# A vision-transformer block: one projection for two groups of tokens, factor products by high and low parts, and a new order of the steps

## The chip, the cores and the metric

The kernel runs on one core of a Trainium2 chip. The metric is the device time of one execution in microseconds (us), lower is better. The engines are TensorE (PE, with its weight loads as PEld), VectorE (DVE), ScalarE (ACT), GpSimd (POOL) and SyncE (SP), which issues most DMAs. A measurement of this kernel can tell about 0.5% from no change.

## The reference

The block takes 32 images of 3x96x96. It cuts each into 36 patches of 768 numbers, projects them to 256 (with a class token: 37 tokens an image, 1184 in all), applies a factored attention, and then a mixture of 8 experts of which each token takes 2. Cut to what matters:

```python
h = concat([cls, patches @ W.T + b], 1) + pos_enc                  # 32 x 37 x 256
x = layernorm(h)
Q, K, Z = x @ Wq.T, x @ Wk.T, cumsum(x, 1) / counts
bil = (Q @ V_b) * cumsum(K @ W_b, 1) @ U_b.T
tri = (Q @ V_t) * (Z @ X_t) * cumsum(K @ W_t, 1) @ U_t.T
h = h + ((bil + alpha * tri) / counts + bias_b + alpha * bias_t) @ Wo.T
x = layernorm(h)
gates = softmax(x @ w_router + b_router)                           # top 2 of 8, 185 places an expert
out = gelu(buf @ w1 + b1) @ w2 + b2                                # for each expert
h = h + weighted sum of each token's two experts, weights divided by their sum
```

## The kernel before

**Groups.** The 1184 tokens lie in ten tiles of 128 (the last has 32). They go through the front part in four groups, `GROUPS` at L26: A (tiles 0 to 2), B (3 to 5), C (6 and 7) and E (8 and 9). In the code they are 0, 1, 2 and 3. `ENDS` and `PATCHES` (L31 and L32) say how many whole images are projected for each group: 11, 10, 7 and 4, that is 396, 360, 252 and 144 columns of patches.

**Units of TensorE.** `UNITS` (L281) is a table of (step, group, slot of PSUM), written by hand, in which TensorE does its work. For each group the steps are `proj` (patches to h), `norm1` (h turned, tokens to rows, so that means and variances can be taken), `xn_t` (the normalised rows turned back), `zc` (two factor products, for Z and for K), `a` (one factor product, for Q), `y` (the product with U and Wo), `norm2` (turned again, with the router's logits), then `slots` (which place each token gets) and `pick` (the first expert's rows). A slot is two of the eight banks. `claim` waits until what lay in the slot is read. The first group's `norm1` is issued inside B's projection (after its third block of six).

**The other engines** have tables too. `DVE_ORDER`: `proj` adds the table of positions to PSUM's sum and writes h; `stats1` and `rstd1` take the statistics of `norm1`'s rows; `sums` are the running sums; `prod`; `add_up` writes the second h; `rstd2`, `choose` (top 2 by MAX and FIND_INDEX), `place` (the one-hot rows), `count`. `ACT_ORDER`: `root1` is the square root between `stats1` and `rstd1`; `norm1` writes the normalised rows; `xn_copy` takes the turned rows out of PSUM. Every engine works through its table in order, and a step that waits holds up all behind it.

**So one group's chain** is: PE `proj`, DVE `proj`, PE `norm1`, DVE `stats1`, ACT `root1`, DVE `rstd1`, ACT `norm1`, PE `xn_t`, then a copy, then PE `zc` and `a`.

**By parts.** Some products are made of float32r operands: a value is split in a high part (a copy on ACT) and a low part (a subtraction on DVE), and three products (high by high, low by high, high by low) are summed. Before, the projections of B and C (`SPLIT`) and the factor products of B (`PARTED`) are made so; for B, ACT's `xn_high` and DVE's `xn_low` take the place of `xn_copy`. All others are float32. In the trace a float32 matmul is two instructions, one by parts is one. `m_high` on ACT and three subtractions on POOL split the three factors.

**Fillers.** `BRIDGES` (L28) puts matmuls whose result nobody reads (of `mean_mat`, L1146) ahead of `slots` 0 and `pick` 0.

**Loads.** SP queues the loads in one order: `first_t` in three pieces, vectors, attention's weights, B's patches, constants, C's patches, E's patches, the first expert's w1 and w2 (L387 to L395). The second expert's weights follow once the last projection is in PSUM, since they overwrite the patches.

**The experts** follow from L1299 on: the first, a look-up of marks (L1096) that gives the rows to gather, and a loop over the rest (L1287, L1322, L1324).

Of the kernel before, what the change touches and what calls it, by code (L numbers as in the profile page):

```python
# [10 lines left out]
D = 256  # L11
# [25 lines left out]
PARTED = (1,)  # L37
# [60 lines left out]
def vit_block(nc, first, patches, const, vectors, attn, w1, w2, b2_rows, xrows, out):  # L98
# [6 lines left out]
    with ExitStack() as ctx:  # L105
# [22 lines left out]
        def spread(per_choice, tiles, n, p=TT):  # L128
# [25 lines left out]
        xn_h, xn_l = (t[:, :, :].rearrange("p k n -> p (k n)")[:, 0:KD * EVEN].rearrange("p (k n) -> p k n", k=KD)  # L154
                      for t in (patch_h, patch_l))
# [12 lines left out]
        hid_hl = sb("hid_hl", [128, KF, 2, SL], f32r)  # L168
        out_t, out_low = held(KF + 2 * KD, KD), held(KF + 3 * KD, KD)
# [61 lines left out]
        def bank(b):  # L231
# [49 lines left out]
        UNITS = [("proj", A, 0), ("mac", 0, 1), ("uw", 0, 2), ("norm1", A, 0), ("proj", B_, 3), ("proj", C, 1),  # L281
                 ("norm1", B_, 2), ("xn_t", A, 0), ("proj", E, 3), ("norm1", C, 1), ("xn_t", B_, 0), ("zc", A, 2),
                 ("zc", B_, 3), ("a", A, 0), ("a", B_, 1), ("norm1", E, 2), ("xn_t", C, 3), ("y", A, 0), ("zc", C, 3),
                 ("y", B_, 1), ("xn_t", E, 2), ("norm2", A, 0), ("zc", E, 3), ("norm2", B_, 2), ("a", E, 1), ("a", C, 3),
                 ("y", E, 1), ("y", C, 3), ("norm2", E, 0), ("slots", 0, 1), ("norm2", C, 2), ("pick", 0, 3),
                 ("slots", 1, 1), ("pick", 1, 3)]
# [4 lines left out]
        DVE_ORDER = [("proj", A), ("uw", 0), ("proj", B_), ("proj", C), ("stats1", B_), ("rstd1", B_), ("proj", E),  # L291
                     ("stats1", C), ("xn_low", B_), ("rstd1", C), ("sums", A), ("sums", B_), ("prod", A), ("stats1", E),
                     ("prod", B_), ("rstd1", E), ("add_up", A), ("sums", C), ("add_up", B_), ("sums", E), ("rstd2", A),
                     ("prod", E), ("prod", C), ("rstd2", B_), ("add_up", E), ("choose", 0), ("add_up", C), ("place", 0),
                     ("count", 0), ("rstd2", E), ("rstd2", C), ("choose", 1), ("below", 0), ("place", 1), ("count", 1)]
        ACT_ORDER = [("mac", 0), ("root1", A), ("norm1", A), ("m_high", 0), ("xn_copy", A), ("root1", B_), ("norm1", B_),
                     ("xn_high", B_), ("root1", C), ("norm1", C), ("xn_copy", C), ("root1", E), ("norm1", E), ("xn_copy", E),
                     ("means2", A), ("squares2", A), ("keep2", A), ("root2", A), ("means2", B_), ("squares2", B_),
                     ("root2", B_), ("rows2", A), ("rows2", B_), ("keep2", B_), ("means2", E), ("keep2", E), ("squares2", E),
                     ("root2", E), ("means2", C), ("squares2", C), ("root2", C), ("rows2", E), ("rows2", C), ("keep2", C)]  # L300
# [218 lines left out]
        def _(act):  # L519
# [86 lines left out]
            for kind, n in ACT_ORDER:  # L606
# [17 lines left out]
                elif kind == "xn_high":  # L624
                    p = filled(act, "xn_t", n).rearrange("p (k s) -> p k s", k=KD)
                    w = group_width(n)
                    copy(xn_h[:, :, 0:w], p[:, :, 0:w]).then_inc(xn_high, 1)
# [76 lines left out]
        def _(dve):  # L704
# [160 lines left out]
            for kind, n in DVE_ORDER:  # L865
# [22 lines left out]
                elif kind == "xn_low":  # L888
# [3 lines left out]
                    dve.tensor_tensor(xn_l[:, :, 0:w], p, xn_h[:, :, 0:w], ALU.subtract).then_inc(dve_drained, 1)  # L892
# [195 lines left out]
        def _(pe):  # L1088
# [32 lines left out]
            def factor_product(dst, n, m, factor):  # L1121

                products = [(factor, xn_t[n % 2])]
                if n in PARTED:
                    products = [(m_h[:, m], xn_h), (m_l[:, m], xn_h), (m_h[:, m], xn_l)]
# [44 lines left out]

            for u, (kind, n, _slot) in enumerate(UNITS):
                if (kind, n) == ("norm1", A):
                    continue
# [24 lines left out]
                elif kind == "proj":  # L1198
                    nb = PATCHES[n][1] - PATCHES[n][0]
                    if n in SPLIT:  # L1200
# [13 lines left out]
                        pieces = []  # L1214
                    elif n == 0:
                        src, pieces = first_t[:, :, D:], PIECES
                    else:
                        src, pieces = wide(patch_t[:, slice(*patch_cols(n))], KP), [(0, KP)]
                        pe.wait_ge(patch_in[n], 16)
                    for i, (a, b) in enumerate(pieces):  # L1220
                        if n == 0:
                            pe.wait_ge(first_in[i], 16)
                        for d in range(KD):
                            for k in range(a, b):
                                ins = pe.matmul(p[:, d * 512:d * 512 + nb * NP2], tok_wt[:, k, d * 128:(d + 1) * 128],  # L1225
                                                src[:, k, :], start=k == 0, stop=k == KP - 1)
                elif kind in ("norm1", "norm2"):
                    ins = rows_turned(kind, n)
                elif kind == "xn_t":
                    drained(pe, "norm1", n)  # L1230
                    t0, c = GROUPS[n]
                    if n == E:
                        pe.wait_ge(pool_set, 9)
                    for i in range(c):
                        for k in range(KD):
                            ins = pe.transpose(p[:, k * 512 + i * TT:k * 512 + (i + 1) * TT],
                                               xn[:, t0 + i, k * 128:(k + 1) * 128], ident)
# [190 lines left out]
```

## Time and profile before

| | |
|---|---|
| median of 3 runs | 160.95 us (160.54 to 161.43) |
| the profiled execution | 159.94 us |
| its span in the trace | 158.1 us, clock of TensorE 0.999 |
| PE, PEld, DVE, ACT, POOL busy | 149.5, 139.4, 103.4, 82.1, 50.8 us |
| the chain that ended last | PE 69%, DMA 9%, DVE 8%, issue 4%, ACT 3% |

All durations below are those of the one profiled execution. 1.8 us of its 159.94 us lie outside its span. The chain is followed back from the last instruction, at each step to what released it. Where PE's lines stand one behind another in it, PE waited for nothing.

### The profile page before, as it was taken

What the parts mean: (1) busy time and instruction counts of PE and PEld (TensorE: products, weight loads), DVE (VectorE), ACT (ScalarE), POOL (GpSimd) and SP (SyncE); (2) the same over time, 40 slices, a digit from 0 to 9 for tenths busy, and PEclk for the clock granted to TensorE, in tenths of its full rate; (3) what the DMA queues carried; (4) which work ended last, traced back from release to release, by engine and by line L of the source; (5) the groups of instructions that cost most, each with busy time, mean ns of one, the idle gap of its engine ahead of it and who ended that gap; (6) DMA issues with size and microseconds to landing.
All of it is one profiled execution on the core that took longest, in us unless ns stands there. A gap on an engine that the chain in (4) does not pass through costs nothing.

```text
span 158.1 us, 3015 instructions
## 1 busy us (share of the span) xinstructions
PE 149.5 (95%) x1010; PEld 139.4 (88%) x1010; DVE 103.4 (65%) x331; ACT 82.1 (52%) x210; POOL 50.8 (32%) x55
## 2 busy tenths in 40 slices
PE   7999999999999889999999999999999999999950
PEld 7559999978788788899799899999999999999950
DVE  0076874579766988981396859669486795794710
ACT  4215544640528989657055657474582665737100
POOL 6003005007230000004537158085372661604351
PEclk9999999999999999999999999999999999999999
DMA  5999960079002273100489887788868988600421
GB/s 173 420 427 406 405 221 0 0 252 326 8 0 92 100 249 130 51 0 26 106 335 298 269 265 185 266 202 300 280 117 281 264 249 255 139 8 0 52 25 23
DMA packets 17123, 28.48 MB, mean 180 GB/s; under 512 B 1149, under 2 KB 13607, under 8 KB 16857
## 3 DMA queue, kind: packets, MB, share of 16 engines
q1 hardware_dynamic: 14649, 25.49, 47.0%
q0 software_dynamic: 2464, 2.86, 10.3%
q8 instruction: 6, 0.10, 0.3%
q14 instruction: 4, 0.03, 0.1%
HBM read 24.21 MB, written 4.14 MB: 179 GB/s over the span
## 4 chain that ended last, share of the span: by engine, by line
PE 69%; DMA 9%; DVE 8%; issue 4%; ACT 3%; POOL 2%; POOLq 1%; SPq 1%; DVEq 0%; ACTq 0%
PE ps L1287 18%; PE ps L1322 10%; PE ps L1225 7%; PE ps L1207 6%; PE ps L1129 6%; DMA w_even<-w 5%; PE ps L1324 4%; PE ps L1162 3%; DMA out_rows<-out_s,dst_row 3%; PE ps L1141 2%; POOL out_rows L496 2%; PE ps L1167 2%; PE ps L1299 2%; DMA rows_in<-xrows,src_row 2%; PE ps L1250 2%
## 5 line engine op out<-in xcount | busy, mean ns | idle before, releaser
L496 POOL DMA_INDIRECT out_rows<-out_s,dst_row x16 | 23.8, 1485 | 38.6 <-ACT out_s L681 32.2
L657 ACT ACTIVATE first_t<-ps,b_cur 128x186 f32<-128x186 f32 x64 | 23.0, 413 | 23.7 <-PE ps L1287 22.1
L1322 PE MATMUL ps<-hid_hl,split 128*128 128x372 f32 x96 | 29.1, 370 | 0.0
L1324 PE MATMUL ps<-hid_hl,split 128*128 128x186 f32 x96 | 23.8, 248 | 0.0
L1287 PE MATMUL ps<-first_t,patch_t 128*128 128x186 f32 x128 | 21.7, 322 | 0.1
L975 DVE CAST hid_hl<-first_t 128x372 fp32r<-128x372 f32 x28 | 10.7, 383 | 15.8 <-ACT first_t L657 15.8
L1287 PEld LDWEIGHTS ps<-first_t,patch_t 128*128 128x128 f32 x128 | 20.1, 190 | 0.4 <-issue 0.4
L481 POOL DMA_INDIRECT rows_in<-xrows,src_row x14 | 15.6, 1112 | 12.9 <-DVE src_row L943 9.0
L1287 PE MATMUL ps<-first_t,w_even 128*128 128x186 f32 x112 | 18.9, 321 | 0.0
L1324 PEld LDWEIGHTS ps<-hid_hl,split 128*128 128x128 f32 x96 | 18.3, 191 | 0.0
L521 ACT ACTIVATE split<-patch_t 128x512 fp32r<-128x512 f32 (+2 forms) x28 | 13.7, 552 | 8.8 <-DMA patch_t<-patches 5.1
L1322 PEld LDWEIGHTS ps<-hid_hl,split 128*128 128x128 f32 x96 | 18.0, 188 | 0.0
L1287 PEld LDWEIGHTS ps<-first_t,w_even 128*128 128x128 f32 x112 | 17.6, 190 | 0.0
L977 DVE TENSOR_TENSOR hid_hl<-first_t,hid_hl 128x372 fp32r<-128x372 f32 x28 | 15.3, 547 | 1.0
L564 ACT ACTIVATE xn<-ps,nmr,rstd 128x256 f32<-128x256 f32 (+1 forms) x20 | 9.7, 556 | 2.2 <-DVE nmr L740 2.2
L1207 PE MATMUL ps<-split 128*128 128x360 f32 (+1 forms) x72 | 10.6, 305 | 0.0
L983 DVE TENSOR_TENSOR split<-patch_t,split 128x512 fp32r<-128x512 f32 x16 | 10.2, 684 | 0.0
L1207 PEld LDWEIGHTS ps<-split 128*128 128x128 f32 x72 | 10.2, 188 | 0.0
L521 ACT ACTIVATE first_t<-ps 128x186 f32<-128x186 f32 x13 | 4.2, 322 | 10.7 <-PE ps L1324 9.7
L1225 PE MATMUL ps<-first_t 128*128 128x396 f32 x24 | 8.5, 510 | 0.0
L983 DVE TENSOR_TENSOR split<-w_even,split 128x512 fp32r<-128x512 f32 x12 | 7.7, 685 | 0.9 <-ACT split L521 0.9
L1225 PEld LDWEIGHTS ps<-first_t 128*128 128x128 f32 x24 | 4.5, 197 | 3.5 <-DMA first_t<-first 0.7
(175 smaller groups left out, 268.8 us busy)
## 6 DMA issues: line engine op xcount, KB each, us to landing
w_even<-w SPq DMA_DIRECT2D x8, 1024.0 KB, 5.7
patch_t<-w SPq DMA_DIRECT2D x8, 1024.0 KB, 5.3
att<-attn SPq DMA_DIRECT2D x1, 1280.0 KB, 8.5
patch_t<-patches SPq DMA_DIRECT2D x1, 1080.0 KB, 10.7
first_t<-first SPq DMA_DIRECT2D x1, 978.0 KB, 6.1
out_rows<-h SPq DMA_DIRECT2D x2, 384.0 KB, 2.9
xrows<-xn SPq DMA_DIRECT2D x2, 384.0 KB, 2.6
patch_t<-patches SPq DMA_DIRECT2D x1, 756.0 KB, 12.1
```

The lines of the kernel that those rows point to most:

```text
L481: pool.indirect_dma_start(out=rows_in[q][0:SIZES[s], s, :], out_offset=None, in_=xrows[:, :], in_offset=bass.IndirectOffsetOnAxis(ap=src_r ...
L496: pool.indirect_dma_start(out=out[:, :], out_offset=bass.IndirectOffsetOnAxis(ap=dst_row[0:SIZES[s], c:c + 1], axis=0), in_=out_s[q][0:SIZ ...
L521: return act.activation(dst, src, ACT.Copy)
L657: ins = act.activation(hid[:, f, :], bank(pair)[:, (f % 2) * SL:(f % 2 + 1) * SL], ACT.Gelu, bias=b1_cur[q][:, f:f + 1])
L975: dve.tensor_copy(hid_hl[:, f, 0], hid[:, f]).then_inc(hid_high, 1)
L977: dve.tensor_tensor(hid_hl[:, f, 1], hid[:, f], hid_hl[:, f, 0], ALU.subtract).then_inc(hid_split, 1)
L983: dve.tensor_tensor(w2_l[q][:, f], w2_s[q][:, f], w2_h[q][:, f], ALU.subtract).then_inc(w2_split, 1)
L1207: ins = pe.matmul(p[:, d * 512:d * 512 + nb * NP2], w[:, k, d * 128:(d + 1) * 128], x[:, k, 0:patch_width(n)], start=k + m == 0, stop=k == ...
L1225: ins = pe.matmul(p[:, d * 512:d * 512 + nb * NP2], tok_wt[:, k, d * 128:(d + 1) * 128], src[:, k, :], start=k == 0, stop=k == KP - 1)
L1287: ins = pe.matmul(bank(pair)[:, (f % 2) * SL:(f % 2 + 1) * SL], w1_s[q][:, k, f * 128:(f + 1) * 128], buf_t[q][:, k, :], start=k == 0, sto ...
L1322: pe.matmul(dst[:, 0:2 * SL], w2_h[q][:, f, cols], hid_hl[:, f].rearrange("p a s -> p (a s)"), start=f == 0, stop=False)
L1324: ins = pe.matmul(dst[:, 0:SL], w2_l[q][:, f, cols], hid_hl[:, f, 0], start=False, stop=f == KF - 1)
```

## The change

- `ENDS` makes three pieces of patches of four: 11, 11 and 10 images become 11, 10 and 11. The third and the fourth projection are one of 396 columns, by parts, and group E's `norm1` waits for that projection.
- Group A's rows are turned back (`xn_t` A, in a new function `turned_back`) inside that projection, after its third block.
- `PARTED` is (0, 1): A's three factor products are by parts as well. Its parts lie in `hid_hl`, which the experts use much later.
- The tables of PE, DVE and ACT are in a new order, and 2 and 2 fillers stand where 4 and 3 stood.

```diff
-BRIDGES = {('slots', 0): 4, ('pick', 0): 3}
+BRIDGES = {('slots', 0): 2, ('pick', 0): 2}
-ENDS = [0] + [min(B, -(-(t0 + n) * TT // T)) for t0, n in GROUPS]
+ENDS = [0] + [-(-(t0 + n) * TT // T) for t0, n in GROUPS[:2]] + [B]
-PARTED = (1,)
+PARTED = (0, 1)
...
+        flat_parts = hid_hl[:, :, :, :].rearrange("p f a s -> p (f a s)")
+        xn_parts = {0: [wide(flat_parts[:, i * KD * EVEN:(i + 1) * KD * EVEN]) for i in range(2)],
+                    1: [wide(t[:, :, :].rearrange("p k n -> p (k n)")[:, 0:KD * EVEN]) for t in (patch_h, patch_l)]}
...
-        UNITS = [("proj", A, 0), ("mac", 0, 1), ("uw", 0, 2), ("norm1", A, 0), ("proj", B_, 3), ("proj", C, 1),
+        UNITS = [("proj", A, 0), ("mac", 0, 1), ("uw", 0, 2), ("norm1", A, 0), ("proj", B_, 3), ("xn_t", A, 3),
...
                 if kind == "norm1":
-                    drained(pe, "proj", n)
+                    drained(pe, "proj", min(n, C))
...
+                            if (n, k) == (C, INSIDE):
+                                claim(PLACE["xn_t", A])
+                                turned_back(A).then_inc(psum_filled, 1)
...
                 elif kind == "a":
+                    drained(pe, "xn_t", n)
+                    if n in PARTED:
+                        pe.wait_ge(m_split, 3)
                     ins = factor_product(p[:, 0:512], n, 0, m_a)
```

**TensorE, from the third projection to the first factor product.** L1207 and L1224 are the projections by parts, L1162 and L1166 `norm1`, L1236 and L1184 `xn_t`, L1225 the float32 projection, L1129 the factor products. Before (after group A's `norm1`):

```order
L1207 MATMUL ps<-split 128x360 x18
L1207 MATMUL ps<-split 128x252 x36
L1162 MATMUL ps<-cst,h_t 128x128 x6
L1236 MATMUL ps<-cst,xn 128x128 x6
L1225 MATMUL ps<-patch_t,first_t 128x144 x12
L1162 MATMUL ps<-cst,h_t 128x128 x4
L1236 MATMUL ps<-cst,xn 128x128 x6
L1129 MATMUL ps<-xn_t,att 128x384 x2
```

Now:

```order
L1224 MATMUL ps<-split 128x360 x18
L1224 MATMUL ps<-split 128x396 x18
L1184 MATMUL ps<-cst,xn 128x128 x6
L1224 MATMUL ps<-split 128x396 x18
L1166 MATMUL ps<-cst,h_t 128x128 x6
L1184 MATMUL ps<-cst,xn 128x128 x6
L1166 MATMUL ps<-cst,h_t 128x128 x4
L1133 MATMUL ps<-hid_hl,m_h 128x384 x2
```

Between B's `norm1` (x6) and B's `xn_t` (x6) stood A's `xn_t`, E's projection and C's `norm1`. Now nothing stands between them.

**VectorE, the same place.** L882 and L884 write h, L719 and L721 are `stats1`, L731 and L733 `rstd1`. Before:

```order
L882 TENSOR_TENSOR h_t<-ps,table 128x10x36 x2
L882 TENSOR_TENSOR h_t<-ps,table 128x7x36 x2
L719 BN_STATS bn<-ps 128x6 x3
L722 BN_AGGR mv<-bn 128x2 x3
L731 RECIPROCAL rstd<-std 128x3
```

Now, with A's `xn_low` (L895) and the larger `proj` behind the statistics of B:

```order
L884 TENSOR_TENSOR h_t<-ps,table 128x10x36 x2
L721 BN_STATS bn<-ps 128x6 x3
L724 BN_AGGR mv<-bn 128x2 x3
L733 RECIPROCAL rstd<-std 128x3
L742 SCALAR_TENSOR_TENSOR nmr<-mv,rstd 128x3
L895 TENSOR_TENSOR hid_hl<-ps,hid_hl 128x768
L884 TENSOR_TENSOR h_t<-ps,table 128x11x36 x2
L895 TENSOR_TENSOR split<-ps,split 128x768
```

C's `proj` stood ahead of `stats1` B and stands behind it now; so does the new subtraction.

**VectorE, ahead of the first choice and behind it.** L803 and L805 are `add_up`, L787 and L789 begin `choose`, L815 and L817 `place`. Before:

```order
L803 SCALAR_TENSOR_TENSOR h_t<-ps,bias_o,h_t 128x160 x2
L787 MAX top<-logit 128x8 x6
L789 SCALAR_TENSOR_TENSOR floored<-top,logit 128x48
L790 SCALAR_TENSOR_TENSOR top<-top 128x6
L792 MAX_INDEX which<-top,floored 128x8 x6
L794 TENSOR_TENSOR is_one<-cst,which 128x96
L796 TENSOR_TENSOR chosen<-is_one 128x48
L803 SCALAR_TENSOR_TENSOR h_t<-ps,bias_o,h_t 128x256 x2
L815 SCALAR_TENSOR_TENSOR place<-ps,chosen 128x6
```

Now:

```order
L805 SCALAR_TENSOR_TENSOR h_t<-ps,bias_o,h_t 128x256 x2
L789 MAX top<-logit 128x8 x6
L791 SCALAR_TENSOR_TENSOR floored<-top,logit 128x48
L792 SCALAR_TENSOR_TENSOR top<-top 128x6
L794 MAX_INDEX which<-top,floored 128x8 x6
L796 TENSOR_TENSOR is_one<-cst,which 128x96
L798 TENSOR_TENSOR chosen<-is_one 128x48
L733 RECIPROCAL rstd<-std 128x1
L733 RECIPROCAL rstd<-std 32x1
```

C's `add_up` (128x256 x2) stands ahead of the first choice, and E's `rstd2` behind it, where `add_up` stood.

## Rows read from the trace of the kernel before

**Rows 1.** Stretches: us, busy us of each engine, clock, DMA share, GB/s.

```profile
27.10:32.50 5.40, 5.40 (x48) 5.35 (x46) 3.51 (x14) 2.58 (x5) 0.14 (x1) 1.00 0.09 5
...
53.30:66.10 12.80, 11.73 (x96) 10.72 (x96) 11.32 (x81) 11.09 (x31) 0.09 (x1) 1.00 0.49 161
```

**Rows 2.** Chain that ended last: start us, us, what, from the second projection on.

```profile
16.22 3.08 PE ps L1207 x18
...
19.96 7.15 PE ps L1207 x54
27.11 0.66 PE ps L1162 x6
27.76 0.66 PE ps L1236 x6
28.41 2.94 PE ps L1225 x24
31.36 0.44 PE ps L1162 x4
31.80 0.69 PE ps L1236 x6
32.48 7.04 PE ps L1129 x30
...
40.39 1.29 PE ps L1250 x4
...
46.94 1.19 PE ps L1129 x8
```

**Rows 3.** VectorE, in order of time: start us, us, line, operation, idle before.

```profile
27.14 0.75 DVE L882 TENSOR_TENSOR h_t<-ps,table 128x252 f32<-128x252 f32 x2 [2.31 <-PE ps L1207]
27.81 1.09 DVE L719 BATCH_NORM_STATS2 bn<-ps 128x6 f32<-128x256 f32 x3
```

**Rows 4.** ScalarE, in order of time.

```profile
17.42 0.41 ACT L521 ACTIVATE split<-patch_t 128x252 fp32r<-128x252 f32 x1 [0.62 <-PE ps L1207]
...
23.26 1.46 ACT L564 ACTIVATE xn<-ps,nmr,rstd 128x256 f32<-128x256 f32 x3
24.61 0.42 ACT L521 ACTIVATE m_h<-m_a 128x256 fp32r<-128x256 f32 x1
...
30.02 1.48 ACT L564 ACTIVATE xn<-ps,nmr,rstd 128x256 f32<-128x256 f32 x3 [0.44 <-DVE nmr L740]
```

**Rows 5.** DMA issues: tile, queue, KB each, us to landing; then the issue in time.

```profile
patch_t<-patches SPq DMA_DIRECT2D x1, 432.0 KB, 12.7
...
4.23 0.94 SPq L387 DMA_DIRECT2D patch_t<-patches  x2
```

**Rows 6.** Chain that ended last, from B's `norm2` to the first expert.

```profile
49.97 0.20 ACT read_s L521
...
53.41 0.43 DVE top L787 x6
...
55.63 0.80 DVE h_t L803 x2
...
60.26 0.38 DVE top L787 x4
...
66.16 0.87 PE ps L1299 x4
```

**Rows 7.** VectorE, the last `rstd2` ahead of the second choice.

```profile
59.58 0.17 DVE L731 RECIPROCAL rstd<-std 128x2 f32<-128x2 f32 x1 [0.79 <-ACT std L533]
```

**Rows 8.** PE, groups by shape: the same matmul in the first 4 us and later.

```profile
L1141 PE MATMUL ps<-mean_mat 128*128 128x128 f32 x12 | 2.9, 434 | 1.0 <-POOL mean_mat L441 1.0
L1146 PE MATMUL ps<-mean_mat 128*128 128x128 f32 x14 | 2.1, 288 | 0.0
```

**Rows 9.** Stretches at the end, columns as in Rows 1.

```profile
152.00:153.00 1.00, 0.46 (x4) 0.22 (x2) 0.48 (x1) 0.00 (x0) 0.62 (x1) 1.00 0.00 0
...
157.00:158.00 1.00, 0.00 (x0) 0.00 (x0) 0.00 (x0) 0.00 (x0) 0.00 (x0) 0.85 0.00 0
```

More of the change, by code:

```diff
@@ L287, in vit_block @@
         PLACE = {(kind, n): u for u, (kind, n) in enumerate(unit[:2] for unit in UNITS if unit[0] != "pick")}
         PICK_SLOT = 3
[L291 to L295, printed above, removed]
@@ L296, in vit_block @@
-        ACT_ORDER = [("mac", 0), ("root1", A), ("norm1", A), ("m_high", 0), ("xn_copy", A), ("root1", B_), ("norm1", B_),
+        DVE_ORDER = [("proj", A), ("uw", 0), ("proj", B_), ("stats1", B_), ("rstd1", B_), ("xn_low", A), ("proj", C),
+                     ("xn_low", B_), ("stats1", C), ("sums", A), ("rstd1", C), ("sums", B_), ("prod", A), ("stats1", E),
+                     ("rstd1", E), ("add_up", A), ("prod", B_), ("sums", C), ("add_up", B_), ("rstd2", A), ("sums", E),
+                     ("prod", E), ("prod", C), ("add_up", E), ("rstd2", B_), ("add_up", C), ("choose", 0), ("rstd2", E),
+                     ("place", 0), ("count", 0), ("rstd2", C), ("choose", 1), ("below", 0), ("place", 1), ("count", 1)]
@@ L1124, in factor_product @@
                 if n in PARTED:
[L1125 removed]
+                    high, low = xn_parts[n]
+                    products = [(m_h[:, m], high), (m_l[:, m], high), (m_h[:, m], low)]
                 width = EVEN if n in PARTED else group_width(n)
@@ L1169, in rows_turned, with turned_back @@
                 return ins
+            def turned_back(n):
+                p = slot("xn_t", n)
+                drained(pe, "norm1", n)
+                t0, c = GROUPS[n]
+                if n == E:
+                    pe.wait_ge(pool_set, 9)
+                for i in range(c):
+                    for k in range(KD):
+                        ins = pe.transpose(p[:, k * 512 + i * TT:k * 512 + (i + 1) * TT],
+                                           xn[:, t0 + i, k * 128:(k + 1) * 128], ident)
+                return ins
             for u, (kind, n, _slot) in enumerate(UNITS):
-                if (kind, n) == ("norm1", A):
+                if (kind, n) in (("norm1", A), ("xn_t", A)):
                     continue
@@ L1213, in _ @@
                                 rows_turned("norm1", A).then_inc(psum_filled, 1)
-                        pieces = []
-                    elif n == 0:
-                        src, pieces = first_t[:, :, D:], PIECES
-                    else:
[L1218 to L1221, printed above, removed]
+                            if (n, k) == (C, INSIDE):
+                                claim(PLACE["xn_t", A])
+                                turned_back(A).then_inc(psum_filled, 1)
+                    else:
+                        for i, (a, b) in enumerate(PIECES):
                             pe.wait_ge(first_in[i], 16)
[L1223 to L1226, printed above, removed]
+                            for d in range(KD):
+                                for k in range(a, b):
+                                    ins = pe.matmul(p[:, d * 512:d * 512 + nb * NP2], tok_wt[:, k, d * 128:(d + 1) * 128],
+                                                    first_t[:, k, D:], start=k == 0, stop=k == KP - 1)
                 elif kind in ("norm1", "norm2"):
@@ L1229, in _ @@
                 elif kind == "xn_t":
[L1230 to L1237, printed above, removed]
+                    ins = turned_back(n)
                 elif kind == "zc":
```

25 lines of the change are left out of this document (13 added, 12 removed).

## The prediction

> **What bounds the kernel now.** I read the busy times of stretches first, then the chain of work that ended last, then VectorE and ScalarE in order of time around the places that the change touches. In the stretch from 27.1 to 32.5 PE is busy for all of its 5.4 us at the full clock [rows 1]. The chain says the same of the whole front part: from 19.96 to 49.9 us it consists of PE rows that follow one another without a gap (ten of them are shown) [rows 2]. So there a microsecond of PE work is a microsecond of time, and a wait of PE is one too. After that DVE and ACT decide: the chain goes from ACT's read at 49.97 over the first choice (53.41) and the second (60.26) to the first expert's matmul at 66.16 [rows 6]. In 53.3 to 66.1 DVE is busy 11.3 of 12.8 us [rows 1]. What follows is the look-up, the gather and the loads that it releases, and the experts; all of it hangs on that matmul and on DVE's work beside it, and nothing there is fixed in time. So I count what the change does to the 66.16, and pass it on one to one.
>
> **PE's work in the projections.** E's float32 projection goes: 2.94 us [rows 2]. C's grows from 252 to 396 columns. The 54 instructions of the second half of B's and of C's projection take 7.15 us, and 18 instructions of 360 columns 3.08 us, or 171 ns each [rows 2]. That leaves 4.07 us for 36 instructions of 252 columns, 113 ns each. No row has 396 columns by parts. The nearest are the 171 ns at 360 columns and the 176 ns at 384 (below); I take 182 ns, 6.55 us in all. The bounds are 113 ns (4.1 us) and, from the same columns in float32 at twice the passes, far more than 200 ns; the near rows leave 175 to 190. So C's projection gains 2.48 us, and both together save 0.46 us.
>
> **PE's work in the factor products.** The 30 instructions of L1129 from 32.48 on take 7.04 us: 12 in float32 and 18 by parts, all of 384 columns [rows 2]. Four float32 instructions of this width take 1.29 us [rows 2], so the 12 take 3.87 us and the 18 take 3.17 us, or 176 ns each. One product is 1.29 us in float32 and 6 x 0.176 = 1.06 us by parts. Three of A's change: 0.70 us saved. The fillers stand in waits and cost nothing before; two and one fewer save nothing by themselves. PE's own work so shrinks by 1.2 us. If PE's queue stayed full, that would be the gain.
>
> **It does not stay full.** B's chain of statistics is the point of this prediction. Before, DVE writes C's h from 27.14 to 27.8 and starts B's statistics at 27.81 [rows 3]; ACT's normalised rows end at 30.02 + 1.48 = 31.50 [rows 4]. That is 3.69 us from the first statistics to the last row. Beside it PE did A's `xn_t` (0.66), E's projection (2.94) and C's `norm1` (0.44), 4.04 us [rows 2], and so B's `xn_t` followed at 31.80 with no wait. In the new order B's `xn_t` stands right behind B's `norm1`: A's `xn_t` and the E columns are ahead of both, C's `norm1` is behind. Nothing covers the chain.
>
> Step by step: C's projection starts at 19.96 + 3.08 = 23.04 as before. It needs 6.55 us and A's `xn_t` inside it 0.66, so B's `norm1` starts at 30.25 (27.11 before) and has been issued at 30.91. Its last result lands 0.2 us later and DVE, idle since the start of C's projection, begins the statistics at 31.12. They don't wait for C's h now, but they could not begin earlier. The rows are there at 31.12 + 3.69 = 34.8. **PE waits from 30.9 to 34.8, 3.9 us.** Behind the waiting instruction on PE stand C's `norm1`, A's and B's factor products and all the rest; A's parts, for one, could have been ready before: only DVE's subtraction for A waits behind B's statistics (33.2 to 34.2), so that A's products could not go ahead either.
>
> **What else moves here, at no cost.** ACT splits the factors ahead of A's normalised rows now. Before, these began at 23.26 and the factors' copies (1.03 us for three) at 24.61 [rows 4]; now the rows begin at about 24.3 and end at 25.8. PE wants them after three blocks, at 23.04 + 3.27 = 26.3: 0.5 us of cover, and if it were gone the wait would be longer by as much. The two last pieces of patches become one transfer, which is needed whole. Before, E's piece landed at 4.7 + 12.7 = 17.4 [rows 5], and ACT first wanted C's patches at 17.42 [rows 4]. So the new transfer lands as it is wanted; a few tenths late would be hidden by the 5.6 us until PE reads that block. The copies and subtractions of 396 columns lie in the same cover.
>
> **From there to the first choice.** From B's `xn_t` (31.80) to the end of B's `norm2` PE took 18.1 us without a wait. Now C's `norm1` is in it (+0.44), half of the L1129 row at 46.94 as well, since E's `a` goes ahead of B's `norm2` (+0.60) [rows 2], and A's products save 0.70. With 0.1 us of small waits: 34.83 + 18.1 + 0.44 = 53.4, against 49.95: 3.45 us late. ACT is busy with A's second rows until then (they have been moved ahead), and reads at 53.6. Squares, root and B's `rstd2` take what they took. Then DVE does C's `add_up` (0.80) [rows 6] where it did E's (0.59), and a little queues up in front; the first choice starts at 57.2 instead of 53.4, 3.8 us late.
>
> **What the new tail gives back.** From the first choice to the second 6.9 us pass now [rows 6]. C's `add_up` (0.80) is no longer between them [rows 6], and DVE's wait of 0.79 us for C's root [rows 7] goes, since `norm2` of C now stands ahead of `slots`. So the second choice starts at 57.2 + 5.3 = 62.5, against 60.26: 2.2 us late, and the 5.9 us from there to the first expert [rows 6] stay. What is late next is ACT's root of C, 0.1 us ahead of DVE: there is no more to be had there. **Sum: +2.2 us.** The profiled execution would be 159.94 + 2.2 = 162.1 us, its span 160.3. The median of the runs lies 1.0 us above the profiled execution, so 160.95 + 2.2 = 163.1 us.
>
> **The bounds of this.** Downward: DVE's 11.3 us of work between the first choice and the expert, less 0.8 for `add_up`, can't be done in less than 10.5 us, so at most 12.8 - 10.5 = 2.3 of the 3.8 us come back: +1.5. At 175 ns for an instruction of 396 columns another 0.25 goes: +1.3. Upward: 190 ns (+0.3), the cover of A's rows gone (+0.3), and two small waits in the tail that I took as met (+0.4): +3.2. With 0.4 us of scatter this is 161.9 to 164.5.
>
> **Rival 1: the clock falls in the wait.** Nothing in the trace of before has a wait of PE like this one ahead of it. At the end of the trace PE's last work is at 152.5 [rows 9] and the granted clock falls within 157 to 158, five microseconds and more later [rows 9]. A wait of 3.9 us is shorter than that, which speaks against it. If it fell, the matmuls after 34.8 would run at the lower level, as in the first 4 us, where the same matmul takes 434 ns against 288 later [rows 8]. With 2 to 4 us of work at half speed that costs 1 to 2 us more: 164.6. The Trainium skill ("TensorE: Matmul & The Clock Gate", section on HAM oscillation) says that idle gaps between the matmuls let the array's clock drop to its lower level; by it the time would be these 164.6 us. I give the case 0.13.
>
> **Rival 2, the other side: PE's saving decides.** If the wide instructions cost what the narrow ones do (113 ns), C's projection would be 2.5 us shorter, all that follows would move up with it, and the sum would be -0.3 us: 160.7. From about 120 ns on it is no longer slower. For it speaks only that no row has this width, and that a part of the cost may be per instruction. Against it, 396 columns in 113 ns would be 3.5 columns a ns, where the rows have 2.2 at most. The same end would come if the wait were under 1.7 us instead of 3.9; its chain has measured times. 0.05.
>
> **Rival 3: the wait is real, but its price is mostly given back,** because what I took as DVE's limit from the first choice on is loose: +0.5, 161.4. The fillers and small waits of PE in this stretch speak for it, DVE's 11.3 of 12.8 us against it. 0.08.
>
> **Chances.** Forecast 0.74, rival 1 0.13, rival 2 0.05 (mostly faster), rival 3 0.08 (mostly same). About 0.5% is what a measurement can tell from no change: slower 0.88, same 0.08, faster 0.04. The range takes the forecast's own, the nearer half of rival 1, and a part of rival 3: 161.5 to 165.0 us.
>
> **What the profile would show.** Right: a PE wait of about 3.9 us ahead of B's `xn_t` (L1184) with ACT's rows as its releaser, near 31 to 35 us; 36 instructions of 396 columns in 6.5 us; the 36 instructions of A's and B's products at 176 ns; the first choice at 57.2, the second at 62.5, the first expert at 68.4; PE busy down by 1 to 2 us and the clock at 1.0. Wrong: a wait under 2 us there, a first expert before 67, a clock under 1 between 35 and 40, or the extra time lying behind the first expert, in loads or gathers, which I passed on unchanged.

## The result, and the profile after

The change made the kernel slower. The median of six runs is 164.31 us (163.63 to 165.33) against 161.1 us (160.54 to 161.43) in six runs of the kernel before: a ratio of 1.021, interval 1.016 to 1.026. In every comparison below a single run that lies over 1.5% above the fastest of its kernel is left out of the ratio.

| | before | after |
|---|---|---|
| the profiled execution, us | 159.94 | 163.63 |
| its span, us | 158.1 | 161.8 |
| mean clock of TensorE | 0.999 | 0.982 |
| PE, PEld, DVE, ACT, POOL busy, us | 149.5, 139.4, 103.4, 82.1, 50.8 | 149.8, 140.8, 105.4, 82.9, 51.2 |

The chain of work that ended last, kernel after, from the second half of B's projection on (start us, us, what):

```profile
20.58 6.22 PE ps L1224 x36
26.80 0.66 PE ps L1184 x6
27.46 3.24 PE ps L1224 x18
30.70 0.67 PE ps L1166 x6
...
31.39 1.10 DVE bn L721 x3
...
32.52 0.33 DVE mv L724 x3
...
32.87 0.31 ACT std L531
...
33.20 0.19 DVE rstd L733
...
33.41 0.17 DVE nmr L742
...
33.61 1.49 ACT xn L566 x3
...
35.23 0.85 PE ps L1184 x6
36.08 0.44 PE ps L1166 x4
36.51 5.75 PE ps L1133 x24
42.27 0.44 PE ps L1166 x4
42.70 2.13 PE ps L1133 x12
```

Before, this stretch was one PE row behind another [rows 2]. Now the chain leaves PE at 31.37 and walks through the whole statistics of group B: statistics, root, reciprocal, normalised rows. It comes back to PE at 35.23. A second thing is to be read in the last rows: 24 factor instructions take 5.75 us, 240 ns each, and 12 of the same width and kind take 2.13 us, 178 ns each. The same instruction became slow and then quick again.

PE in order of time, kernel after (the bracket: idle time before the row, and what ended it):

```profile
35.23 0.85 PE L1184 MATMUL ps<-cst,xn 128*128 128x128 f32 x6 [3.87 <-ACT xn L566]
...
36.92 0.84 PE L1133 MATMUL ps<-hid_hl,m_l 128*128 128x384 f32 x2
...
40.35 0.52 PE L1133 MATMUL ps<-split,m_l 128*128 128x384 f32 x2
```

Stretches, kernel after (us, busy us of PE, PEld, DVE, ACT, POOL, granted clock, DMA share, GB/s):

```profile
31.00:35.00 4.00, 0.35 (x4) 0.12 (x2) 3.18 (x11) 1.69 (x4) 0.00 (x0) 1.00 0.79 265
35.00:36.00 1.00, 0.77 (x7) 0.81 (x8) 0.40 (x1) 0.08 (x1) 0.00 (x0) 1.00 1.04 358
36.00:37.00 1.00, 1.00 (x8) 1.00 (x7) 0.00 (x0) 0.81 (x1) 0.00 (x0) 0.71 1.08 366
...
38.00:39.00 1.00, 1.00 (x5) 1.00 (x4) 0.90 (x4) 0.03 (x1) 0.00 (x0) 0.50 0.47 152
39.00:40.00 1.00, 1.00 (x5) 1.00 (x4) 0.00 (x0) 0.27 (x1) 0.00 (x0) 0.58 0.00 0
40.00:41.00 1.00, 1.00 (x7) 1.00 (x7) 0.80 (x1) 0.00 (x0) 0.00 (x0) 1.00 0.00 0
```

PE idles, then works again, and 1.2 us after it has begun the clock falls to 0.50, the level of 1.2 GHz, until about 39.8. PE is busy for all of that time, so the busy share hides the loss. What was lost is the fall summed over the stretch: 0.29 + 0.50 + 0.50 + 0.42 = 1.7 us by the clock's column (the row of 37 to 38 also stands at 0.50). By the instructions it is 36 x 0.176 = 6.34 us of factor work [rows 2] against 5.75 + 2.13 = 7.88 in this chain: 1.54 us. I call it 1.6.

The front's end, kernel after (DVE, then PE, in order of time):

```profile
59.30 0.49 DVE L789 MAX8 top<-logit 128x8 f32<-128x8 f32 x6
...
64.56 0.37 DVE L789 MAX8 top<-logit 128x8 f32<-128x8 f32 x4
```

```profile
70.46 1.81 PE L1309 MATMUL ps<-first_t,w_even 128*128 128x186 f32 x10 [0.25 <-DVE first_t L965]
```

These answer to 53.41, 60.26 and 66.16 [rows 6]. One correction is needed first. The second projection, which the change does not touch, began at 16.08 us in the profiled execution of before and at 16.71 in that of after; over the profiles of all kernels here it began between 16.07 and 17.48, whatever the kernel. The difference arises in the 24 instructions of the first projection (8.39 us of PE work before, 9.03 after, the clock's column at 1.00 in both); why they vary, no run here shows. So I count from there:

| kernel | second projection | first choice | second choice | first expert | projection to expert | against before |
|---|---|---|---|---|---|---|
| before | 16.08 | 53.32 | 60.26 | 66.16 | 50.08 | |
| after | 16.71 | 59.30 | 64.56 | 70.46 | 53.75 | +3.67 |

### The profile page after: what moved, and what is told of

Its sections match the earlier page's. It is cut to its first block, busy times and chain, and to the rows that moved or that the text cites. A ratio compares the mean times of both kernels' runs of the same rounds, so it can differ in the third digit from the quotient of the medians.

```text
span 161.8 us, 2969 instructions
## 1 busy us (share of the span) xinstructions
PE 149.8 (93%) x986; PEld 140.8 (87%) x986; DVE 105.4 (65%) x330; ACT 82.9 (51%) x210; POOL 51.2 (32%) x55
## 4 chain that ended last, share of the span: by engine, by line
PE 87%; DVE 4%; ACT 3%; issue 2%; POOLq 1%; POOL 1%; DVEq 0%
PE ps L1297 24%; PE ps L1332 12%; PE ps L1224 8%; PE ps L1133 8%; PE ps L1239 6%; PE ps L1334 5%; PE ps L1318 3%; PE ps L1260 3%; PE ps L1166 3%; PE ps L1342 2%; PE ps L1120 2%; PE ps L1145 2%; ACT xn L566 2%; PE ps L1309 2%; PE ps L1171 2%; PE ps L1285 2%
## 5 line engine op out<-in xcount | busy, mean ns | idle before, releaser
L523 ACT ACTIVATE split<-patch_t 128x512 fp32r<-128x512 f32 (+2 forms) x28 | 14.4, 578 | 8.9 <-DMA patch_t<-patches 5.1
L1224 PE MATMUL ps<-split 128*128 128x360 f32 (+1 forms) x72 | 13.2, 338 | 0.0
L1224 PEld LDWEIGHTS ps<-split 128*128 128x128 f32 x72 | 12.3, 188 | 0.0
L1239 PE MATMUL ps<-first_t 128*128 128x396 f32 x24 | 9.2, 543 | 0.0
L471 POOL TENSOR_TENSOR z_s<-first_t,z_s 64x384 f32<-64x384 f32 (+1 forms) x3 | 2.8, 921 | 18.3 <-DVE first_t L845 18.3
L1239 PEld LDWEIGHTS ps<-first_t 128*128 128x128 f32 x24 | 5.0, 213 | 3.7 <-issue 0.9
```

The costliest lines, as they stand in the source:

```text
L523: return act.activation(dst, src, ACT.Copy)
L1224: ins = pe.matmul(p[:, d * 512:d * 512 + nb * NP2], w[:, k, d * 128:(d + 1) * 128], x[:, k, 0:patch_width(n)], start=k + m == 0, stop=k == ...
```

## Experiments

Eleven kernels ran, one of them the changed kernel again. The theory: the statistics of group B have lost their cover and PE waits for them; the clock falls on account of that wait; both go if B's `norm1` is put where something covers it. The rivals: the wider projection itself costs more, A's parts cost instead of saving, the new tail is at fault, or the low clock comes from something other than the idle time.

**The change unaltered, again.**

> The changed kernel itself, unaltered, on the same chip as the two others here. Expected: the clock falls behind the wait again, mean clock 0.97 to 0.987, ratio to the kernel before 1.02. A mean clock of 0.99 or more in a run would say that the fall is a matter of chance.

Measured: 165.22 us (164.47 to 165.62, 4 runs), before 161.47 (16 runs), ratio 1.022 (1.016 to 1.027). The stretches of its profile:

```profile
31.00:35.00 4.00, 0.98 (x8) 0.71 (x6) 2.54 (x10) 1.06 (x3) 0.00 (x0) 0.91 0.54 187
35.00:36.00 1.00, 0.14 (x1) 0.17 (x2) 1.00 (x3) 0.71 (x2) 0.00 (x0) 0.50 1.00 391
...
40.00:41.00 1.00, 1.00 (x5) 1.00 (x4) 0.23 (x2) 0.30 (x1) 0.00 (x0) 0.50 0.00 0
```

The wait is 3.87 us again. The fall came earlier this time, while PE still idled, and lasted until 41; of that, the five microseconds of PE's work from 36 to 41 at half rate cost 2.5. Of the ten runs of the changed kernel two have a profile, and the fall stands in both. The other eight have only a mean clock. Nine of the ten means lie at 0.969 to 0.982, under every run of the kernel before in these groups (0.986 to 0.998); the tenth, 0.987 with 164.45 us, can't be told from them. So a fall comes in at least nine of ten; where it lies in the eight without a profile isn't seen, and in the two profiles it begins at different times. Among the first six, the runs with 0.97 are about 1.6 us longer than two with 0.982 (165.25 and 165.33 against 163.63 and 163.72).

**Fillers in the wait** (15 of them, so that PE has work of about 3.5 us and the wait itself stays).

```diff
-BRIDGES = {('slots', 0): 2, ('pick', 0): 2}
+BRIDGES = {('slots', 0): 2, ('pick', 0): 2, ('xn_t', 1): 15}
```

> The changed kernel with 15 filler matmuls (float32, 128 columns, result read by nobody) ahead of B's `xn_t`, in PE's wait of 3.87 us. They take about 3.3 us, so the wait stays filled and B's `xn_t` starts no later. Theory (the wait costs about 2.2 us by itself, and the granted clock of 0.50 from 36.3 to 39.6 costs another 1.6 us): the clock stays at 1.00, the idle time ahead of B's `xn_t` is about 0.6 us, and the time is 164.3 - 1.6 = 162.7 us. Rival (the clock's fall is covered by other waits and costs nothing): 164.3 us, with the clock at 1.00 all the same.

Measured: 163.0 us (162.41 to 164.88, 4 runs), before 160.84 (13 runs), ratio 1.011 (1.005 to 1.017). PE, its profile:

```profile
31.82 3.51 PE L1150 MATMUL ps<-mean_mat 128*128 128x128 f32 x30
35.77 0.88 PE L1184 MATMUL ps<-cst,xn 128*128 128x128 f32 x6 [0.43 <-ACT xn L566]
```

The clock stayed at 1.00 from 31 to 40 us and three of four runs came out at 162.4 to 163.4, 0.9 to 1.9 us under the changed kernel's 164.31. The fourth is the profiled one, and it has a fall of another kind:

```profile
60.00:62.00 2.00, 1.22 (x15) 0.96 (x14) 1.86 (x17) 2.00 (x7) 0.00 (x0) 0.89 0.05 12
62.00:64.00 2.00, 2.00 (x8) 2.00 (x9) 1.93 (x13) 1.97 (x9) 0.00 (x0) 0.50 0.57 197
64.00:66.00 2.00, 2.00 (x12) 2.00 (x11) 1.86 (x18) 1.98 (x6) 0.00 (x0) 0.76 0.51 169
```

Here PE was busy 1.22 of 2 us, waiting around the two thinned-out rows of fillers (0.30 and 0.48 us). The fall doesn't always come there: the profile of after has the same two waits, 0.30 and 0.48 us, with the clock at 1.00. The profile of the kernel with a better order, further down, has nearly the same two (0.31 and 0.47 us), PE busy for 1.22 of 2 us from 56 to 58, and a clock of 1.00. So this is a second place where the clock can fall. Whether the 2 and 2 fillers in place of 4 and 3 make it one, the next run looks at.

**Fillers in the wait, and 4 and 3 of them again in the tail.**

```diff
-BRIDGES = {('slots', 0): 2, ('pick', 0): 2}
+BRIDGES = {('slots', 0): 4, ('pick', 0): 3, ('xn_t', 1): 15}
```

> The changed kernel with 15 fillers in the wait, and ahead of `slots` 0 and `pick` 0 the 4 and 3 fillers of the kernel before where the change has 2 and 2. In one run of the kernel with 15 fillers and 2 and 2 the clock fell to 0.50 near 61 to 65 us, and two of the six runs of the changed kernel have a mean clock of 0.97 and 165.3 us against 0.982 and 163.7. Theory (the thin fillers let the clock fall a second time in some runs): every run has a mean clock of 0.99 or more and lies within 0.6 us of 162.7 us. Rival (the fall there has another cause): one run or more again with a clock under 0.985 and 1.5 us longer.

Measured: 163.31 us (162.75 to 163.84, 4 runs), before 161.21 (23 runs), ratio 1.015 (1.009 to 1.021). The mean clock was 0.990 to 0.996 in all four. Two of the four, 163.65 and 163.84 us, still lie further from 162.7 than the 0.6 us expected. From the second projection to the first expert 52.62 us pass, +2.54 against before. The last fillers stand behind a wait of 0.48 us and not in it, and from the second choice to the expert 6.06 us pass instead of the changed kernel's 5.90. So the added fillers cost about 0.16 us of it. The rest is the wait's own price with the clock out of it. Where one run of four fell before, none of four did; it fits, and four runs are few.

**The projection merged, nothing else** (kernel before; `ENDS` of after, so that pieces of 11, 10, 7 and 4 images become 11, 10 and 11, and E's projection taken out of the tables of PE and DVE).

```diff
-ENDS = [0] + [min(B, -(-(t0 + n) * TT // T)) for t0, n in GROUPS]
+ENDS = [0] + [-(-(t0 + n) * TT // T) for t0, n in GROUPS[:2]] + [B]
...
-                 ("norm1", B_, 2), ("xn_t", A, 0), ("proj", E, 3), ("norm1", C, 1), ("xn_t", B_, 0), ("zc", A, 2),
+                 ("norm1", B_, 2), ("xn_t", A, 0), ("norm1", C, 1), ("xn_t", B_, 0), ("zc", A, 2),
```

> The kernel before with the merged projection alone: 11, 10 and 11 images, the third projection of 396 columns by parts, E's float32 projection gone; A's products in float32, A's `xn_t` behind B's `norm1` as before, all tables otherwise as before. Theory: C's projection takes 6.5 us, B's chain has only A's `xn_t` and C's `norm1` (1.1 us) beside it and VectorE writes C's h ahead of it, so PE waits 3.1 us ahead of B's `xn_t`: +2.7 us, 163.8 us; if the clock falls, 165.3 us. Rival (the merged projection is good and A's parts or the new tables cost the time): 160.6 us.

Measured: 163.57 us (163.47 to 163.86, 4 runs), before 160.84, ratio 1.016 (1.01 to 1.021). PE, and the stretch behind the wait, its profile:

```profile
35.63 0.85 PE L1236 MATMUL ps<-cst,xn 128*128 128x128 f32 x6 [2.97 <-ACT xn L564]
```

```profile
36.00:38.00 2.00, 2.00 (x11) 1.34 (x10) 0.57 (x1) 0.99 (x2) 0.00 (x0) 1.00 1.09 365
```

The merge alone opens most of the wait: 2.97 us, and +2.59 us from the second projection to the expert. The 2.94 us of E's float32 projection [rows 2] had been the cover, and moving its columns ahead of B's `norm1` took it away. The clock did not fall: its means are 0.996 and 0.997 in all four runs. So the wait of 2.97 us in this kernel leaves the clock alone, and the one of 3.87 in the changed kernel does not.

**The order alone, the projections as before** (kernel before, with A's `xn_t` and E's projection ahead of B's `norm1`, and C's `norm1` behind B's `xn_t`).

```diff
-                 ("norm1", B_, 2), ("xn_t", A, 0), ("proj", E, 3), ("norm1", C, 1), ("xn_t", B_, 0), ("zc", A, 2),
+                 ("xn_t", A, 0), ("proj", E, 3), ("norm1", B_, 2), ("xn_t", B_, 0), ("norm1", C, 1), ("zc", A, 2),
```

> The kernel before with two units moved and nothing else: A's `xn_t` and E's projection go ahead of B's `norm1` instead of behind it, C's `norm1` behind B's `xn_t`. The same work, the same fillers, no product changed. Theory (the cover of B's chain of statistics is what the change gave up): PE waits 3.9 us ahead of B's `xn_t`, the clock falls behind it for about 3.3 us, and the time is 161.1 + 3.9 + 1.6 = 166.6 us. Rival (the cost lies in the merged projection and its parts): within 1 us of 161.1.

Measured: 166.53 us (166.23 to 167.59, 4 runs), before 160.84, ratio 1.036 (1.030 to 1.043). PE, and a stretch, its profile:

```profile
35.70 1.17 PE L1236 MATMUL ps<-cst,xn 128*128 128x128 f32 x6 [3.88 <-ACT xn L564]
```

```profile
36.00:38.00 2.00, 2.00 (x11) 1.85 (x9) 0.24 (x1) 0.81 (x1) 0.00 (x0) 0.52 1.08 370
```

With no wider projection, no parts for A and the old tail, the same wait (3.88 us) and the same fall are there. It is the order of PE's table that makes both: two units ahead of B's `norm1` and one behind B's `xn_t`. There is nothing in this kernel to set against them, so it is slower than the changed one.

**A's products by parts, nothing else** (kernel before).

```diff
-PARTED = (1,)
+PARTED = (0, 1)
```

> The kernel before with A's three factor products by parts alone (their parts in the experts' buffer, as in the changed kernel); the projections, the order and the fillers as before, with ScalarE's `xn_high` A for `xn_copy` A and VectorE's `xn_low` A behind B's `rstd1`. Theory (each product saves 0.23 us and nothing else moves): the stretch of factor products from B's `xn_t` on is 0.7 us shorter, 18 + 18 instructions at 176 ns; 160.84 - 0.7 = 160.1 us. Rival (VectorE's added subtraction, 0.96 us, delays E's h or C's statistics and eats it): 160.8 us.

Measured: 160.81 us (159.78 to 161.39, 12 runs), before 161.21 (23 runs), ratio 0.998 (0.995 to 1.001). PE, then DVE, its profile:

```profile
35.65 0.59 PE L1131 MATMUL ps<-split,m_h 128*128 128x384 f32 x2 [0.30 <-DVE split L893]
```

```profile
34.59 0.96 DVE L893 TENSOR_TENSOR split<-ps,split 128x768 fp32r<-128x768 f32 x1 [0.96 <-ACT split L522]
```

The 0.70 us did not arrive here; 0.2 to 0.4 did, within what can't be told from nothing. A's products end earlier, and then PE waits for the low part of B, which DVE can only subtract once ACT has copied the high part. The saving is real as work and is worth its full price only where the next group's parts are ready sooner.

**B's `norm1` inside the merged projection** (the changed kernel; A's `xn_t` goes behind it, and DVE's and ACT's tables follow).

```diff
-                 ("proj", C, 1), ("norm1", B_, 2), ("xn_t", B_, 0), ("norm1", C, 3), ("zc", A, 2), ("zc", B_, 1),
+                 ("proj", C, 1), ("xn_t", A, 3), ("xn_t", B_, 0), ("norm1", C, 3), ("zc", A, 2), ("zc", B_, 1),
...
                             if (n, k) == (C, INSIDE):
-                                claim(PLACE["xn_t", A])
-                                turned_back(A).then_inc(psum_filled, 1)
+                                claim(PLACE["norm1", B_])
+                                rows_turned("norm1", B_).then_inc(psum_filled, 1)
```

> The changed kernel with B's `norm1` issued inside the merged projection (after its third block) where A's `xn_t` was, and A's `xn_t` right behind the projection. All work and both kinds of parts stay as in the changed kernel; VectorE does C's `proj` ahead of A's `xn_low`, ScalarE B's `root1` and `norm1` ahead of A's `xn_high`. Theory (the wait and the clock are the whole cost, the saving of 1.2 us of PE work is real): the second half of the projection covers B's chain, PE waits at most 1.4 us (for C's h), the clock stays at 1.00, the first expert starts 0.4 us ahead of the kernel before: 160.7 us. Rival (the merged projection and the parts cost something of their own): above 162 us though the wait is gone.

Measured: 159.93 us (159.31 to 161.44, 10 runs), before 160.84, ratio 0.996 (0.992 to 1.000). PE, its profile:

```profile
26.63 0.82 PE L1166 MATMUL ps<-cst,h_t 128*128 128x128 f32 x6
27.21 3.50 PE L1224 MATMUL ps<-split 128*128 128x396 f32 x18
30.54 1.63 PE L1184 MATMUL ps<-cst,xn 128*128 128x128 f32 x12
33.32 0.66 PE L1166 MATMUL ps<-cst,h_t 128*128 128x128 f32 x4 [1.15 <-DVE hid_hl L895]
```

Now 3.5 us of projection stand between B's `norm1` and B's `xn_t`, and the twelve turned-back instructions follow without a gap. The clock stays at 1.00. From the second projection to the expert the kernel is 0.37 us shorter than before, where after was 3.67 longer. The new places of two steps, with DVE's and ACT's tables to match, are worth 4.04 us, and the rest of the change is kept: the wide projection, A's parts, the new tail. Together those three cost nothing against the kernel before; what each is worth by itself this kernel doesn't say. The ratio is within what can't be told from no change. A wait of 1.15 us is left, ahead of C's `norm1`: C's h stands behind A's subtraction.

**A better order from there** (C's `norm1` ahead of B's `xn_t`, C's statistics ahead of B's subtraction, ACT's last rows and copies in another order).

```diff
-                 ("proj", C, 1), ("xn_t", A, 3), ("xn_t", B_, 0), ("norm1", C, 3), ("zc", A, 2), ("zc", B_, 1),
+                 ("proj", C, 1), ("xn_t", A, 0), ("norm1", C, 3), ("xn_t", B_, 1), ("zc", A, 2), ("zc", B_, 1),
```

> As the kernel with B's `norm1` inside the merged projection, but C's `norm1` ahead of B's `xn_t`, VectorE's statistics of C ahead of B's `xn_low`, and ScalarE's last steps (`rows2` and `keep2` of C and E) in another order. There PE waited 1.15 us for VectorE's `xn_low` A ahead of C's `norm1`. Theory (the wait is on the path): it is split and shorter, 0.6 us, and the first expert starts 0.4 us earlier: 159.93 - 0.4 = 159.5 us. Rival (VectorE decides further on, and the order ahead of it makes nothing): 159.9 us.

Measured: 159.9 us (159.28 to 163.04, 12 runs), before 161.21, ratio 0.993 (0.990 to 0.996). The wait ahead of C's `norm1` is 0.58 us now, and from the second projection to the expert 49.46 us pass, 0.25 less than without this order. The 159.5 us expected did not come; the median is that of the rival, 159.9. But the runs of before beside it are slower too, and the distance to them is 1.31 us, where it was 0.91. The gain is between the theory's 0.4 and nothing, too small to tell. One run of the twelve, the 163.04, had a mean clock of 0.977.

**The same with 4 and 3 fillers.**

```diff
-BRIDGES = {('slots', 0): 2, ('pick', 0): 2}
+BRIDGES = {('slots', 0): 4, ('pick', 0): 3}
```

> The kernel with B's `norm1` inside the projection and the newer order (159.9 us median in 12 runs, one of 163.0 us with a mean clock of 0.977), with the 4 and 3 fillers of the kernel before in place of 2 and 2. Theory (the thin fillers made that one run's clock fall): no run with a mean clock under 0.985; the median stays, 159.9 us, or grows by 0.2 us where a filler outlasts its wait. Rival (chance of another kind): a run as before.

Measured: 160.05 us (159.44 to 161.23, 12 runs), before 161.47 (16 runs), ratio 0.992 (0.989 to 0.995). All twelve means of the clock lie at 0.988 or more. One fallen run of twelve against none of twelve doesn't show that the fillers made the difference. These two are the best kernels found, 0.7 to 0.8% faster than before and about 3% faster than the change as it stands.

**What of the wait drops the clock? Half of it filled, the idle part last.**

```diff
-BRIDGES = {('slots', 0): 2, ('pick', 0): 2}
+BRIDGES = {('slots', 0): 2, ('pick', 0): 2, ('xn_t', 1): 7}
```

> The changed kernel with 7 fillers in PE's wait ahead of B's `xn_t` instead of 15: 1.6 us filled, 2.3 us idle. Theory: the stretch of idle PE is then shorter than in the changed kernel (3.87 us, clock fell) and than in the kernel with the merged projection alone (2.97 us, clock stayed), so the clock stays at 1.00 from 30 to 42 us and the time is that with 15 fillers, 163.0 us. Rival (what matters is how little PE did around the wait, in sum): the clock falls as in the changed kernel, 164.3 us.

Measured: 165.41 us (164.37 to 166.57, 4 runs), before 161.21, ratio 1.030 (1.024 to 1.036). PE, and a stretch, its profile:

```profile
31.34 1.73 PE L1150 MATMUL ps<-mean_mat 128*128 128x128 f32 x14
35.28 0.88 PE L1184 MATMUL ps<-cst,xn 128*128 128x128 f32 x6 [2.22 <-ACT xn L566]
```

```profile
37.00:40.00 3.00, 3.00 (x11) 3.00 (x10) 1.88 (x5) 0.30 (x2) 0.00 (x0) 0.50 0.63 210
```

This expectation failed. The idle part is 2.22 us, shorter than the 2.97 us that did no harm in the merged kernel, and the clock fell in all four runs (means 0.973 to 0.980), in the profile at the same place as without fillers. Seven fillers at the front of the gap buy nothing.

**The idle part first, then fillers** (six of them that wait for B's statistics).

```diff
                 p = slot("xn_t", n)
+                if n == B_:
+                    pe.wait_ge(stats1_ready, 2)
+                    bridge(6, p[:, 512:640])
                 drained(pe, "norm1", n)
```

> The changed kernel with 6 fillers late in PE's wait: they wait for B's `rstd1` on VectorE and end when ScalarE's rows are there. PE idles about 2.3 us first and works for 1.3 us then, the other way round than with 7 fillers at the front, where 2.2 us of idle PE were enough for the clock to fall. Theory (idle time behind the fillers, right ahead of the products, makes the fall): the clock stays at 1.00 from 30 to 42 us, and the time is 163.0 us. Rival (the work missing in the whole wait makes it, wherever the fillers stand): it falls as with 7 fillers in front, 164.5 us or more.

Measured: 163.8 us (162.53 to 165.26, 4 runs), before 161.47, ratio 1.014 (1.005 to 1.023). PE, its profile:

```profile
33.11 1.58 PE L1150 MATMUL ps<-mean_mat 128*128 128x128 f32 x12 [2.37 <-DVE nmr L742]
34.52 0.88 PE L1187 MATMUL ps<-cst,xn 128*128 128x128 f32 x6
```

The four runs are two pairs: 162.53 and 162.76 us at clocks of 0.995 and 0.991, and 164.84 and 165.26 at 0.981 and 0.982. The profile shows one of the first pair, at 1.00 throughout. In the second pair the clock fell somewhere, and the pairs are 2.1 to 2.7 us apart; but no run of the second pair was profiled. The kernel has the thin fillers of the tail too, and the run that fell there, with 15 fillers in the wait, had the same mean clock and time (0.982, 164.88 us). So it isn't shown that these two runs fell at the wait. What is shown is that a gap of 2.37 us with fillers behind it left the clock at 1.00 in the profiled run.

This run also gives the front with a clock of 1.00 and the tail of the change: from the second projection 41.32 us to the first choice, 46.58 to the second, 52.49 to the expert. Against it the changed kernel's 53.75 us are 1.26 us longer. That is what the fall cost at the first expert.

## Why the prediction was right, and where it was not

The forecast was 163.1 us (161.5 to 165.0), the result 164.31. The sign and the mechanism are those of the forecast; the rest of the distance is a rival that came true on top of it. The repeated run came to 165.22 us, above the range; against the runs of before beside it that is +3.75 us, where the forecast had +2.2 and the first six runs had +3.2. The range holds the result because it took in half of rival 1; and 0.6 us of the delay came back behind the first expert, where the forecast had nothing, which is luck. Times of the forecast are compared after the 0.63 us by which the profiled execution began late.

- **The projections.** B's `norm1` was to start at 30.25 and started at 30.70 - 0.63 = 30.07. 18 instructions of 396 columns took 3.24 us, 180 ns each, where I took 182. Rival 2 (113 ns) is out, by this row and by the kernel with B's `norm1` inside.
- **The factor products.** 12 take 2.13 us at full clock, 178 ns each, 176 predicted. That the saving counts one to one where PE's queue is full holds only while DVE's and ACT's parts keep up: alone in the old order it brought 0.2 to 0.4 of its 0.70 us. In the changed kernel the wait gives them the time, so the term stands there.
- **The wait.** 3.9 us predicted, 3.87 measured, ended by ACT's normalised rows, and its chain runs from 31.39 to 35.10, 3.71 us against 3.69 before. The order-only kernel shows that the order of PE's table makes it, the merged kernel that the cover which went was E's projection, and the kernel with B's `norm1` inside the projection that it goes when the cover comes back.
- **The tail.** First choice to second: 5.26 us, 5.3 predicted. Second to first expert: 5.90, 5.9 predicted. So 1.6 of the 6.9 us between the choices came back, as computed. Rival 3 is out: with the clock held by fillers the front is still +2.54.
- **The sum without the clock.** Counted from the second projection at 16.08, the forecast has the first choice at 41.1, the second at 46.4 and the first expert at 52.3 us. The kernel with late fillers, whose profile has a clock of 1.00, has 41.32, 46.58 and 52.49. So without the clock's fall the sum holds within 0.2 us at all three places.
- **The clock: the step that failed.** "A wait of 3.9 us is shorter than that, which speaks against it" put rival 1 at 0.13, and the sum has the clock's fall at nothing. It happened in at least nine runs of ten. Two of the forecast's own signs say so: the clock was under 1 between 35 and 40 us, and PE's busy time rose by 0.3 us where it was to fall by 1 to 2. The first choice came at 59.30 - 0.63 = 58.67 against 57.2 predicted, and the expert at 69.83 against 68.4: 1.5 and 1.4 us, nearly all of the 1.6 that the low clock costs by its column, and near the 1.26 by the kernel with late fillers. My only evidence was the end of the trace of before [rows 9], where the clock fell five microseconds after the last matmul. That is a single row at one place, and it does not say what a gap in the middle of dense work does. In the trace of after the same reading at the end is shorter:

```profile
155.00:157.00 2.00, 1.19 (x11) 0.95 (x9) 0.48 (x1) 0.00 (x0) 0.71 (x1) 1.00 0.39 39
...
159.00:160.00 1.00, 0.00 (x0) 0.00 (x0) 0.00 (x0) 0.00 (x0) 0.00 (x0) 0.65 0.81 92
```

PE's last matmul ends at 156.2 and the clock falls near 159.3, three microseconds later. The size that I gave the rival (1 to 2 us) held, and so did its direction. What it was taken from did not: in the first 4 us, which the forecast calls the lower level, the clock's column reads 1.00. At the lower level of this trace two instructions of 384 columns take 0.84 us and later 0.52.

The Trainium skill ("TensorE: Matmul & The Clock Gate", section on HAM oscillation) says that idle gaps between the matmuls drop the array's clock. The 3.87 us gap agrees in at least nine of ten runs; the 2.97 us gap of the merged kernel, where the clock stayed, shows that not every gap does it.

- **Behind the first expert** I passed the delay on unchanged. The sum of the parts is 0.63 (late start) + 3.67 (front) = 4.30, and the profiled time grew by 3.69, so 0.61 us came back. Most of it came back at one place, at the start of a pass of the experts' loop. First before, then after:

```profile
79.67 0.60 PE L1332 MATMUL ps<-cst,first_t 128*96 128x128 f32 x4
90.53 0.64 PE L1332 MATMUL ps<-cst,first_t 128*96 128x128 f32 x4 [0.30 <-DVE first_t L988]
```

```profile
83.88 0.60 PE L1342 MATMUL ps<-cst,first_t 128*96 128x128 f32 x4
94.29 0.64 PE L1342 MATMUL ps<-cst,first_t 128*96 128x128 f32 x4
```

The delay is 4.21 us at the first pair and 3.76 at the second, and it is 3.73 at PE's last matmul (152.18 and 155.91). Before, PE waited at 90.53 for DVE, and the chain that ended last came there from the load of `w_even`, 7.73 us from 78.26 on: ACT began to split the weights at 86.02. After, the same load was issued at 82.80, 4.54 us later, but ACT began at 89.77, only 3.75 later, and PE didn't wait. So a load that was on the path before was off it after; why it took less time is not shown. The medians grew by 3.2 us (164.31 less 161.1); two profiled executions can't say more about the difference.

**What stays open** is what in PE's work decides the fall. Length of the gap alone is excluded: 2.97 us kept the clock in four runs of four, and 2.22 us behind seven fillers dropped it in four of four (by the mean clocks; one profile each). In the merged kernel A's `xn_t` and C's `norm1` stand between B's `norm1` and the gap, in the others nothing or fillers do. Float32 products of A follow its gap instead of products by parts; but they follow in the order-only kernel too, where the clock fell behind 3.88 us. Either may matter, or where in time the gap lies; no run separates them. Open as well is whether the fall in the tail hangs on the number of fillers.

## What to carry to other kernels

Before a step is moved or merged away, look at what waits beside it: 2.94 us of PE work that looked like the cost was the cover of another engine's 3.7 us chain, and the cure was to issue the start of that chain one step earlier, inside the long product. A gap of PE that a change opens has two prices, its length and the clock behind it, so don't price the second as a rare rival, and look for it in the windows' clock column, since the busy share doesn't show it. A saving of work on the busiest engine is worth its price only up to the next wait, so read who feeds the instruction behind it.

## What the runs showed of the hardware

- The clock can fall after PE has resumed. In the profile of after it is 1.00 through the gap of 3.87 us and falls 1.2 us behind it, in the repeated run it falls inside the gap, near 34.3. It stayed at 0.50 from 36.4 to 39.8 us in the first and from 34.3 to 41.1 in the second, though PE had no idle time from 35.2 and 35.9 on.
- The same kernel can come out in two groups of times that go with its mean clock: 162.5 to 162.8 us at 0.991 to 0.995, and 164.8 to 165.3 us at 0.981 to 0.982.
- Waits of 0.30 and 0.48 us, with PE busy for 1.22 of 2 us, were followed by a fall in one profile (15 fillers) and by none in another (the better order).
- Fillers in a part of the wait are no sure cure: 1.73 us of them ahead of a gap of 2.22 us gave 165.41 us, no better than none (164.31 and 165.22); 1.58 us of them behind a gap of 2.37 us gave 162.5 to 165.3; 3.51 us of them gave 163.0.
